# Row maxima from fp32 score products, and the minus maximum written into the score banks by VectorE

## What is computed

```python
# layer 0, per batch, on the group-normalized x
e1, e2 = conv1x1(x, w1), conv1x1(x, w2)              # 64 x 4096 each, PReLU
asm = conv1x1(x, wa)                                 # 128 x 4096
score = softmax(einsum('nci,ncj->nij', e1, e2), axis=2)
x = x + einsum('nij,ncj->nci', score, asm)
# layer 1, per batch, on layer-normalized tokens
t = tanh(f[:, :, None, :] + g[:, None, :, :] + b1)   # additive attention, causal
e = exp(einsum('bija,a->bij', t, w2) + b2) * tril(-1)
t = t + (e / sum(e)) @ x
# then a gate, the 8 best tokens for each of 64 experts, and two products per expert
```

## Time and profile before

| | |
|---|---|
| median of 3 runs | 6023.43 us (6017.64 to 6026.70) |
| profiled execution, its own time | 6020.11 us |
| its span | 6018.3 us |
| mean granted TensorE clock | 0.955 of full speed |
| TensorE busy | 5277.4 us, 88% |
| ScalarE busy | 4960.0 us, 82% |
| VectorE busy | 2143.0 us, 36% |
| GpSimd busy | 2006.2 us, 33% |

### The profile page before, as it was taken

One profiled execution on the slowest core, in us unless ns is written; L12 is line 12 of the kernel. 1 busy time (PEld: TensorE's weight loads), 2 busy tenths in 40 slices (PEclk: granted clock), 3 DMA queues, 4 the chain that ended last, 5 costly groups with the idle time before them and its releaser, 6 DMA issues. The chain is left out here.

```text
span 6018.3 us, 73524 instructions
## 1 busy us (share of the span) xinstructions
PE 5277.4 (88%) x29484; PEld 1737.6 (29%) x29588; DVE 2143.0 (36%) x3620; ACT 4960.0 (82%) x4234; POOL 2006.2 (33%) x1644
## 2 busy tenths in 40 slices
PE   5999988999999987899999987899999997666657
PEld 1233332223333333222333333222333333111113
DVE  8621237541222246552232236653231225100133
ACT  0027969999998969999978959999986978999970
POOL 0265450124444441113455451112455451111110
PEclk8999999999999999999999999999999999888987
DMA  0000000000000010000000010000000001000028
GB/s 25 1 15 8 11 29 1 1 1 4 8 11 11 11 43 8 1 1 1 8 18 8 11 37 13 1 1 1 8 17 9 8 29 29 1 1 1 6 94 281
DMA packets 35763, 115.87 MB, mean 19 GB/s; under 512 B 5024, under 2 KB 5856, under 8 KB 28320
## 3 DMA queue, kind: packets, MB, share of 16 engines
q1 hardware_dynamic: 34608, 110.78, 5.5%
q10 hardware_dynamic: 816, 0.39, 0.0%
HBM read 81.46 MB, written 29.49 MB: 18 GB/s over the span
## 5 line engine op out<-in xcount | busy, mean ns | idle before, releaser
L879 ACT ACTIVATE tanh_slots<-query_part,key_part 128x2048 f32<-128x2048 f32 (+41 forms) x3072 | 4176.2, 1473 | 176.9 <-DVE key_part L1295 110.2
L947 PE MATMUL ps<-tanh_slots,packed 128*32 128x512 f32 (+2 forms) x18432 | 2075.6, 587 | 428.3 <-ACT tanh_slots L879 418.5
L832 POOL TENSOR_TENSOR context_and_exp_sums<-context_and_exp_sums,exp_scores 128x512 f32<-128x512 f32 (+3 forms) x544 | 633.8, 1185 | 1919.0 <-ACT exp_scores L891 1553.5
L947 PEld LDWEIGHTS ps<-tanh_slots,packed 128*32 128x32 f32 x18432 | 540.4, 113 | 1793.1 <-ACT tanh_slots L879 925.8
L900 ACT ACTIVATE _tokens_second_and_probs<-ps 128x1024 f32<-128x1024 f32 x512 | 542.9, 1060 | 605.1 <-PE ps L975 416.0
L845 POOL TENSOR_TENSOR conv_prob_sums<-conv_prob_sums,_tokens_second_and_probs 128x512 f32<-128x512 f32 x480 | 616.0, 1283 | 1191.6 <-ACT _tokens_second_and_probs L900 1183.7
L985 PE MATMUL ps<-_tokens_second_and_probs,asm_tokens 128*128 128x512 f32 x2048 | 997.9, 613 | 1.8 <-DVE tmp_low L1213 1.8
L1357 DVE TENSOR_REDUCE row_max_parts<-ps 128x1 f32<-128x512 f32 x1024 | 623.8, 681 | 308.8 <-PE ps L1063 308.7
L1207 DVE TENSOR_TENSOR context_and_exp_sums<-context_and_exp_sums,ps 128x512 f32<-128x512 f32 (+3 forms) x544 | 346.2, 639 | 859.5 <-PE ps L958 855.8
L847 POOL TENSOR_TENSOR conv_prob_sums<-conv_prob_sums,_tokens_second_and_probs 128x512 f32<-128x512 f32 x480 | 617.9, 1287 | 37.6
L1191 DVE TENSOR_TENSOR exp_scores<-exp_scores,packed 128x128 f32<-128x128 f32 x128 | 76.4, 597 | 1519.8 <-ACT exp_scores L891 1519.8
(11 more groups left out here) (169 smaller groups left out, 2505.8 us busy)
## 6 DMA issues: line engine op xcount, KB each, us to landing
y_scratch<-residual_chunks SPq DMA_DIRECT2D x64, 256.0 KB, 2.0
...
```

The source lines that it names most:

```text
L832: pool.tensor_tensor(dst, dst, src, ALU.add).then_inc(s_ds, 1)
L879: nc.scalar.activation(S[:, 4 * (R % 2) + k, q:SUP], F[:, SUP * blk.s + q:SUP * blk.s + SUP], ACT.Tanh, bias=keypart(blk.b, kg, kg + 1)).t ...
L947: last = mm(PS[32 * k:32 * k + 32, t, off:CHUNK], w2k[:, g, :], S[:, 4 * (R % 2) + k, CHUNK * t + off:CHUNK * t + CHUNK], start=(g == 0), ...
```

## The change

Stage S is gone. M makes 128 blocks per batch of 128 rows by 1024 keys, each of two fp32 products of 64 rows side by side into two banks, and one maximum over both banks; the blocks go row block by row block. For batch 0 they use banks 4 and 5 once and then 0 to 3, and the maxima leave in four parts, so that conv can start while they run; for the other batches they use banks 4 to 7. `row` saves minus the maximum, in fp32, to DRAM, and `bc` reads it back for each chunk, spread over 128 partitions. For each pair P a new stage NB on VectorE copies that chunk's spread row into the pair's two banks (128 by 1024), after EX of the pair that held them; the short products L975 are gone, and QK adds onto what NB wrote. Two pairs of banks serve pairs 32 to 63 alone. `plan()` has the new stages with their costs, and the rest of the order falls out of it. The core of the diff:

```diff
+NBC = 4
+NPAIR = NBLK * NCH // 2
...
+def parts(b):
+    return 1 if b else 4
+
+def max_banks(b, m):
+    if b:
+        return 4 + 2 * (m % 2)
+    return 2 * (m % 2) if m else 4
+
+def pair_bank(P):
+    return 0 if 2 * PPC <= P < PER * PPC and P % 2 else 4
+
+def pair_before(P):
+    return max((x for x in range(max(0, P - 3), P) if pair_bank(x) == pair_bank(P)), default=None)
...
     def conv(b, cs):
...
-                put("PE", "QK", (P,), 1.25, behind, 4)
+                old = pair_before(P)
+                behind = [("DVE", "NB", P - 1) if P else None, ("ACT", "EX", old) if old is not None else None]
...
+                put("DVE", "NB", (P,), 1.2, behind, 2)
+                put("PE", "QK", (P,), 1.1, [("DVE", "NB", P), ("PE", "QK", P - 1) if P else None], 4)
...
+            put("SP", "bc", a, 0.1, behind, 0, 2.5)
...
     def prep(b):
...
-        for h in range(4):
-            put("ACT", "S", (b, h), 2.9, [prior, ("ACT", "S", b, h - 1) if h else None], 3)
-            put("DVE", "S", (b, h), 3.4, [("ACT", "S", b, h), ("DVE", "S", b, h - 1) if h else None], 4)
-        ring = max_ring(b)
-        for m in range(NCH * NBLK):
-            put("PE", "M", (b, m), 0.48, [("DVE", "S", b, 3), ("PE", "M", b, m - 1) if m else None,
-                                          ("DVE", "M", b, m - len(ring)) if m >= len(ring) else None], 4)
-            put("DVE", "M", (b, m), 0.6, [("PE", "M", b, m), ("DVE", "M", b, m - 1) if m else None], 4)
-        put("DVE", "M0", (b,), 0.5, [("DVE", "M", b, NCH * NBLK - 1)], 3)
...
+        for m in range(NPAIR):
+            behind = [("DVE", "Ev", b, NCH - 1)] + max_free(b) if m == 0 else [("PE", "M", b, m - 1)]
+            put("PE", "M", (b, m), 0.9, behind + [("DVE", "M", b, m - 2) if m >= 2 else None], 4)
+            put("DVE", "M", (b, m), 1.25, [("PE", "M", b, m), ("DVE", "M", b, m - 1) if m else None], 4)
+        for i in range(parts(b)):
+            put("DVE", "M0", (b, i), 0.3, [("DVE", "M", b, NPAIR // parts(b) * (i + 1) - 1)], 3)
...
-                for i in range(3):
-                    for u in range(2):
-                        sp.dma_start(NMR[HALF * u + i:HALF * u + i + 1, :], NMX[:, i, :]).then_inc(s_nmr, 16)
+            def row(b, i):
+                n = NBLK // parts(b)
+                sp.wait_ge(s_wf, at["wf", ("M1", b, i)])
+                rows = p_dram[b][0:1, BLK * n * i:BLK * n * i + BLK * n].rearrange("o (k q) -> (o k) q", q=BLK)
+                sp.dma_start(rows, NM[0:n, :]).then_inc(s_nms, 16)
+
+            def bc(b, c):
+                cc = NCH * b + c
+                sp.wait_ge(s_nms, 16 * (piece(b, c * parts(b) // NCH) + 1))
+                if cc >= NBC:
+                    sp.wait_ge(s_nb, PPC * (cc - NBC + 1))
+                src = p_dram[b][0:1, CHUNK * c:CHUNK * c + CHUNK].to_broadcast([128, CHUNK])
+                sp.dma_start(NMB[:, cc % NBC, :], src).then_inc(s_nmr[cc % NBC], 16)
...
-            def S_(b, h):
-                t = slice(1024 * h, 1024 * h + 1024)
-                act.wait_ge(s_wf, at["wf", ("Ev", b, NCH - 1)])
-                nc.scalar.copy(E1P[0:HALF, t], E1[0:HALF, t]).then_inc(s_eh, 1)
...
             def QK(P):
                 cc, p = P // PPC, P % PPC
-                if p == 0 and cc % NCH == 0:
-                    pe.wait_ge(s_nmr, 96 * (cc // NCH) + 96)
-                free = P - 1 if P < 4 * PPC else P
-                if free > 0:
-                    pe.wait_ge(s_pe, free)
                 c, i = cc % NCH, pair_bank(P)
+                pe.wait_ge(s_nb, P + 1)
                 for u in range(2):
                     h = slice(HALF * u, HALF * u + HALF)
-                    mm(PS[:, i + u, :], E2P[h, BLK * p:BLK * p + BLK], E1[h, CHUNK * c:CHUNK * c + CHUNK],
-                       start=True, stop=False)
-                for u in range(2):
-                    h = slice(HALF * u, HALF * u + 3)
-                    last = mm(PS[:, i + u, :], ONE3[h, :], NMR[h, CHUNK * c:CHUNK * c + CHUNK], start=False, stop=True)
+                    last = mm(PS[:, i + u, :], E2P[h, BLK * p:BLK * p + BLK], E1[h, CHUNK * c:CHUNK * c + CHUNK],
+                              start=False, stop=True, skip_group_check=True)
                 last.then_inc(s_qk, 1)
...
             def M(b, m):
...
-                for e2 in (e2h(b), E2M):
-                    last = mm(PS[:, ring[m % len(ring)], :], E1P[:, BLK * ib:BLK * ib + BLK],
-                              e2[:, CHUNK * h:CHUNK * h + CHUNK], start=(e2 is not E2M), stop=(e2 is E2M))
+                if m >= 2:
+                    pe.wait_ge(s_mxd, NPAIR * b + m - 1)
+                i = max_banks(b, m)
+                for u in range(2):
+                    z = slice(HALF * u, HALF * u + HALF)
+                    last = mm(PS[:, i + u, :], E1[z, BLK * ib:BLK * ib + BLK], E2P[z, CHUNK * h:CHUNK * h + CHUNK],
+                              start=True, stop=True)
                 last.then_inc(s_mxq, 1)
...
-                v.tensor_reduce(MX[:, ib, h:h + 1], PS[:, max_ring(b)[m % len(max_ring(b))], :], AXX, ALU.max).then_inc(s_mxd, 1)
+                v.tensor_reduce(MX[:, ib, h:h + 1], PS[:, i:i + 2, :].rearrange("p a b -> p (a b)"), AXX, ALU.max)\
+                    .then_inc(s_mxd, 1)
...
+            def NB(P):
+                cc, old = P // PPC, pair_before(P)
+                i = pair_bank(P)
+                if P % PPC == 0:
+                    dve.wait_ge(s_nmr[cc % NBC], 16 * (cc // NBC + 1))
+                if old is not None:
+                    dve.wait_ge(s_pe, old + 1)
+                v.tensor_copy(PS[:, i:i + 2, :], NMB[:, cc % NBC, None, :].to_broadcast([128, 2, CHUNK])).then_inc(s_nb, 1)
```

131 lines of the change are left out of this document (57 added, 74 removed).

## The result

The changed kernel takes 6102.8 us (median, 6100.9 to 6107.8) against 6022.3 for the kernel before it on the same chips: ratio 1.0135, 95% interval 1.0117 to 1.0153. It is slower by 80 us; the forecast was 6074, slower, with a range to 6120.

The account below looks back on a forecast made before the run. ScalarE was taken to bound the bodies, TensorE to be full in gaps. Halves 0 +56, half 1 of batch 0 +12, of batches 1 and 2 +54, start -71: +51, so 6074 us median, range 6005 to 6120.

Parts of the forecast that it names:

- What bounds each stretch: Before the change: ScalarE bounds bodies between restart and last context sum; in gaps TensorE is full, 3.30 us per pair.
- the ring: Cycle in a gap: score products, exponential, hop, asm products, then again; 4.17 us per pair against 3.30.
- The cycle in a gap: Asm products precede the next pair's score products, so a pair costs 4.17 us against 3.30; the copy is covered.
- Halves 0: Four halves: gap +21, body -1 (exponential) and -7 (half the idle time), L4 and L5 products +1; +14 each, +56.
- Half 1 of batch 0: Gap from 18.1 to 58 us, +40; body -28 from casts, exponentials and 6 us of idle time; sum +12.
- Half 1 of batches 1 and 2: Gap from 83.2 to 134 us, +51; body -24 from casts, exponentials and 5 us of idle time; +27 each, +54.
- The start: Up to the first tanh: score products begin at about 119, first tanh at 430 instead of 500.7; -71 us.
- The rest: What follows the last gap: the change touches nothing there.
- TensorE bounds the bodies: Rival, chance 0.14: each pair in a body gives 0.32 us more; 5983 us, faster.
- cancellation: Rival, chance 0.12: bodies give back all idle time (15, 16, 21 us), start saves 75; centred at 6025 us.
- The clock in the gaps: Rival, chance 0.12: granted clock 0.85 in gaps, or masks queue behind copies on VectorE; 6137 us, slower still.
- Asm products behind the score products: Rival, no chance of its own: copies run early and hide fully, so a gap pair stays at 3.3 us.

Follow-up runs that it names:

- experiment 1: The changed kernel with each pair's asm products ordered behind the next pair's score products, and the first bank 0 copy after batch 0's maxima: 5982.7 us, ratio 0.9929.
- experiment 2: The changed kernel with a second pair of score banks (0 and 1) for every second pair late in the gaps: 5970.6 us, ratio 0.9908; output differs from the reference.
- experiment 5: The kernel before with only its order changed: from pair 65 on, score products stand behind the previous pair's asm products: 6260.1 us, against 6027.4 beside it.
- experiment 9: The kernel before without its short products, minus the maximum left out of the exponentials, no copies, same order: 5977.0 us, ratio 0.9918.

## Why the prediction was right, and where it was off

*What bounds each stretch: right, with one reading too wide.* That TensorE is full holds for the gaps after half 1. After half 0 of batch 0 it was busy 47.67 of 61.50 us, at a granted clock of 0.86, and the prediction counted every gap by the full one's cycle; the steps it got from that, +22, came out at +19 to +20. The gaps became the ring's; the loss lies there and the gain in the start, in the casts and in the exponentials that left the bodies.

*The cycle in a gap: right.* 4.17 us forecast, 4.17 measured, TensorE waiting for the exponential. Experiments 1, 2 and 5 show that the order of the two products makes it: 3.52 with the score products first, 2.97 with other banks, and 4.48 when the kernel before is given this order.

*Halves 0: the term that failed.* The prediction took a gap of +21, 1 more for L4 and L5, and a body that loses 8, for +14. Measured are gaps of +19.2 to +20.4, and bodies of -0.9, +3.5, -3.3 and -3.3: +18.2, +24.0, +16.4 and +16.6 a half, 75 us for 56. The step "part of its 15 us of ScalarE idle time, since TensorE is relieved; I take half" was wrong. In the four bodies ScalarE was idle 56.8 us and is idle 57.2. Its groups in half 0 of batch 0, after and before (count, busy, mean ns, then idle time before them and its releasers; 4 us ahead of the first tanh belong to the start):

```profile
L910 ACT ACTIVATE tanh_slots<-query_part,key_part 128x2048 f32<-128x2048 f32 (+51 forms) x256 | 275.6, 1179 | 8.9 <-PE ps L971 4.7 <-DVE key_part L1314 4.2
L931 ACT ACTIVATE _tokens_second_and_probs<-ps 128x1024 f32<-128x1024 f32 x46 | 48.0, 1042 | 7.1 <-PE ps L991 7.1
```

```profile
L879 ACT ACTIVATE tanh_slots<-query_part,key_part 128x2048 f32<-128x2048 f32 (+51 forms) x256 | 278.8, 1216 | 11.3 <-PE ps L947 7.4 <-DVE key_part L1295 3.9
L900 ACT ACTIVATE _tokens_second_and_probs<-ps 128x1024 f32<-128x1024 f32 x48 | 51.7, 1077 | 8.0 <-issue 5.9 <-PE ps L975 2.1
```

Tanh waits 4.7 us for TensorE instead of 7.4, the exponential of conv 7.1 instead of 2.1, and behind the last tanh, at the very end of the body, ScalarE idles 2.9 us instead of the 5.9 of the last row. The prediction took the idle time for something spread over the body. It isn't: 15.2 of the 15.4 us lie in the body's last 60, where the tanh are short, and in experiment 9 it is the same, 14.9 of 15.1. ScalarE is the fourth engine of these rows, the kernel before first, then experiment 9:

```profile
787.70:847.70 60.00, 57.12 (x329) 20.44 (x328) 24.18 (x40) 44.77 (x91) 28.57 (x25) 1.00 0.15 53
```

```profile
767.40:827.40 60.00, 54.60 (x311) 19.60 (x310) 24.22 (x39) 45.09 (x91) 28.89 (x25) 1.00 0.15 53
```

In the 287 us ahead ScalarE idles 0.2 us, so a relief of TensorE has nothing to give back there. In the last 60 TensorE has 2.5 us less to do in experiment 9 and gives back 0.3. What those waits hang on was not tried. TensorE's order moves them: ScalarE's idle time in the seven bodies is 119 us before, 112 in the changed kernel, 102 in experiment 1 and 104 in experiment 5.

In sum the bodies became 74.8 us shorter where 108 were forecast, and 28 of the 33 us between are those of the halves 0. The gaps grew by 222.8 where 230 were forecast, and the start and the rest were 4.3 us over: 33.2 - 7.2 + 4.3 = 30 us, which is what the forecast of +51 lacked of +81.

*Half 1 of batch 0.* Gap 58 forecast, 58.7 measured. Body -28 forecast, -23.0 measured: ScalarE is busy 22.3 us less (casts and exponentials), and of its idle time only 0.7 us came back for 6. *Half 1 of batches 1 and 2.* Gap 134 forecast, 133.3 measured. Body -24 forecast, -24.9 and -23.1 measured; here 4.2 and 2.7 us of idle time came back for 5. The relief of TensorE alone doesn't bring that (experiment 9: these bodies grow by about 1 us each); from what it comes was not tried.

*The start.* 430 forecast, 431.2 measured; first score products 119 and 121.9. Some of that is luck: the earlier trace rows give 3.63 / 4 = 0.91 us for a product of a run, not the 0.86 that the sum uses. The rows of the start above have three blocks in 2.77 us where the sum has 2.58, and a pair of score products in 0.86 where it has 1.06. The two errors cancel.

*The rest* grew by 2.8 us, which no term had. The other ten kernels have 1031 to 1037 there, so the changed kernel's 1039.5 is the longest; it was not followed up.

*The rivals.* "TensorE bounds the bodies" and "cancellation" both needed time that TensorE's relief gives back in the bodies: experiment 9 rules it out. "The clock in the gaps": it is 1.00 in the gaps after half 1, and 0.91 to 0.92 after the halves 0. That is under 1.00, which the prediction named as a sign of being wrong, but above the 0.86 to 0.88 of the kernel before. VectorE's masks don't queue either: a mask starts 0.03 us behind its exponential in the median, before and now, and 0.12 us in the mean for 0.06. "Asm products behind the score products" isn't what the change does, and with them the ring is 3.52 us (experiment 1), near the 3.6 that the prediction gave for it and not 3.3; it would still have won.
